# A node pass as two turns of 196 units instead of fourteen turns of 28 (one fused graph layer and mixture-of-experts kernel)

## The chip, the cores and the metric

The kernel runs on one core of a Trainium2 chip. The metric is the device time of one execution in microseconds (us). Before the change it is 3060.57 us, the median of three runs (3055.15 to 3062.44).

## What is computed

The reference takes 50,000 nodes with 768 float32 features and 25,000 edges sorted by destination, and does two things one after the other:

```
x = x + gnn(layernorm(x), src, dst, W, attn_l, attn_r, W_res)   # attention over a node's edges, + residual matmul, relu
x = x + ffn(layernorm(x)[None], moe0_*, A1_*, A2_*, G_W)[0]      # gelu(x @ W1 + b1) @ W2 + b2; 6 class tokens apart
```

The first part has a sum over edges per node (softmax weights over each node's incoming edges) and a matmul with W_res for every node, whose result goes through a relu. The second part is, for all nodes but the first six, an up-projection from 768 to 96, a gelu and a down-projection back to 768. The first six rows go through pairs of small experts with a gate.

## The kernel before, in words

Everything is written by hand for the five engines: each engine has a block of its own (`sync`, `gpsimd`, `scalar`, `tensor`, `vector`) whose instructions run in the order in which they are written, and semaphores join them. There are two passes over data. The edge pass handles 196 chunks of 128 edges in a loop of 14 chunks (`NB` turns), and writes sums per chunk to a table in HBM. A short stretch of single steps joins the sums of chunks. Then comes the node pass, which the change is about.

The node pass has `NT` = 392 units of 128 nodes. `turns(eng, NT // U, 1)` makes its turns, and the inner `for u in range(U)` is written out by Python when the kernel is built. With `U` = 28 there are 14 turns. `turns` gives the first two as Python integers (written out in the program), the rest from 2 on by `eng.Fori`, a loop with a register that all five engines run each for itself, and last a drain turn, again an integer. In the drain only stages that are still behind exist (`exists`). So 12 of the 14 turns are one body of instructions that the engines run 12 times, with 11 jumps back to its start. The body's number of instructions, as the compiled program lists them: ScalarE 183, GpSimd 152, SyncE 153, VectorE 281.

A unit t passes through stages that lie some units apart (`L_BASE` = 3 to `L_ST` = 20), so each engine works on several units at once:

- SyncE loads node rows, two units at a time, into `x_ring` (14 units deep) and transposed ones into `xt_ring` (7 deep), and stores results from `y_ring`.
- GpSimd (lines 550 to 578) prepares `g_ring`, gathers the edge sums of the unit's nodes into it (L570, an indirect DMA; nodes without edges are left out), normalises (L562), and takes reciprocal roots (L578).
- ScalarE copies transposes out of PSUM (L647), takes squares and sums for the norms (L640, L661, L678), and does the gelu (L667).
- VectorE adds the residual and the gathered sums (L1174, L1179), adds the down-projection (L1163), takes norms' statistics (L1202) and splits the hidden values (L1214).
- TensorE does in each unit six transposes (L707), the up-projection (L839), six down-projection matmuls (L851) and six residual matmuls (L860).

In the loop, the number that a semaphore is waited for depends on the turn, so it stands in a register that the engine computes. In written-out turns it is a constant. The relevant helper:

```
    yield 0
    yield 1
    with eng.Fori(2, n) as b:
        yield b
```

Of the kernel before, what the change touches and what calls it, by code (L numbers as in the profile page):

```python
# [16 lines left out]
HC = P // DH  # L17

PAIR = 2
U = 28  # L20
XR = 14
GR = 7
NT = -(-N_NODES // (P * U)) * U
# [28 lines left out]
L_BASE = 3  # L52
L_RES = 4
L_Y = 5
# [14 lines left out]
def turns(eng, n, drain):  # L69


    yield 0
    yield 1
    with eng.Fori(2, n) as b:
        yield b
    for b in range(drain):
        yield n + b

# [11 lines left out]
def at_least(eng, sem, value):  # L90

    if not isinstance(value, int) or value > 0:
        eng.wait_ge(sem, value)


def gnn_ffn_kernel(nc, x, x_cols, edges, dst_next, dst_prev, dst_ends, chunk_base, sel_heads,
# [9 lines left out]
    with ExitStack() as ctx:  # L106
# [283 lines left out]
        @block.sync  # L390
        def _(sp):

            sp.dma_start(ident[:], eye).then_inc(l_const, 16)
            sp.dma_start(w_dup[:, 0:DH], w_gnn).then_inc(l_const, 16)
            sp.dma_start(w_dup[:, DH:P], w_gnn).then_inc(l_const, 16)
            sp.dma_start(attn_sb[:], attn).then_inc(l_const, 16)
            sp.dma_start(wgv[:, :, 0:P], w_gnn_bd[:, None, :].to_broadcast([P, NC, P])).then_inc(l_const, 16)
            sp.dma_start(wr_bd[:], w_res_bd).then_inc(l_const, 16)
            sp.dma_start(w1_sb[:], w1.rearrange("(c p) h -> p c h", p=P)).then_inc(l_const, 16)
            sp.dma_start(b1_sb[:], b1.rearrange("(p a) -> p a", a=1)).then_inc(l_const, 16)  # L400
            sp.dma_start(w2_sb[0:HID, :], w2).then_inc(l_const, 16)
            sp.dma_start(w2_sb[HID:HID + 1, :], b2.rearrange("(a c) -> a c", a=1)).then_inc(l_const, 16)

            sp.dma_start(gw_sb[:], gw.rearrange("(c p) g -> p c g", p=P)).then_inc(l_cls, 16)
            sp.dma_start(a1b_sb[:], a1b).then_inc(l_cls, 16)
            sp.dma_start(cb_sb[:], chunk_base).then_inc(l_fix, 16)

            sp.wait_ge(s_rowinit, 1)
            sp.dma_start(row_d.rearrange("(p n) o -> p (n o)", p=P), row_init).then_inc(d_rowinit, 16)

            for b in turns(sp, NB, 2):
                for i in range(BODY):
                    co_ = BODY * b + i - L_AGG
                    if exists(co_, EC):
                        v = (i - L_AGG) % G
                        sp.wait_ge(s_eo, co_ + 1)
                        sp.dma_start(agg_v[ds(co_, 1)].rearrange("a p d -> p (a d)"), agg_ring[:, v, :])\
                            .then_inc(d_agg[v], 16)

            sp.wait_ge(s_ecol, EC)  # L420
            sp.wait_ge(s_tr, NBLK * EC)
            sp.wait_ge(s_ag, 2 * EC)
            sp.dma_start(row_i, dst_ends.rearrange("(o n) e -> o n e", o=1).to_broadcast([P, 2, EC])).then_inc(l_fix, 16)
            sp.dma_start(sel_sb, sel_heads).then_inc(l_fix, 16)
            sp.wait_ge(s_tab, NG)
            sp.dma_start(tab_d, tab[:]).then_inc(d_tab, 16)
            sp.wait_ge(d_tab, 16)
            for k in range(G):
                sp.dma_start(tb.rearrange("h (g k) n -> h g k n", k=G)[:, :, k, :],
                             tab_d[k * HEADS:(k + 1) * HEADS]).then_inc(l_tab, 16)  # L430
            for u in range(G):
                sp.wait_ge(d_agg[u], 16 * (EC // G))
            sp.dma_start(o_last, tail_v[:, :, P - 1, :]).then_inc(d_last, 16)
            for u in range(2):
                sp.wait_ge(d_scat[u], 16 * (EC // 2))

            for b in turns(sp, NT // U, 1):
                for u in range(U):
                    t = b * U + u
                    if u % PAIR == 0 and exists(t, NT):  # L440
                        v = u % XR
                        j = v // PAIR
                        n = 2 * b + u // XR
                        q = b * (U // PAIR) + u // PAIR
                        at_least(sp, s_y, t - XR + PAIR)
                        settle(sp)
                        sp.dma_start(x_ring[:, v:v + PAIR, :], x_v[ds(q, 1)].rearrange("q p k c -> p (q k) c"))\
                            .then_inc(d_x[j], 16)
                        at_least(sp, d_g[(u - XR) % GR], 16 * (4 * b + (u - XR) // GR + 1))
                        settle(sp)  # L450
                        at_least(sp, d_g[(u - XR + 1) % GR], 16 * (4 * b + (u - XR + 1) // GR + 1))
                        settle(sp)
                        sp.dma_start(nrow[:, v:v + PAIR], row_v[ds(q, 1)].rearrange("q p k -> p (q k)"))\
                            .then_inc(d_x[j], 16)
                    tx = t - L_XT
                    if exists(tx, NT):
                        g = (u - L_XT) % GR
                        at_least(sp, s_res, tx - GR + 1)
                        settle(sp)
                        sp.dma_start(xt_ring[:, g, :], x_cols[ds(tx, 1)].rearrange("t f c -> f (t c)"))\  # L460
                            .then_inc(d_xt[g], 16)
                    if isinstance(t, int) and t == NT + 10:
                        sp.wait_ge(s_y, NT)
                        sp.dma_start(a1_sb, a1w.rearrange("(c p) a h -> p c a h", p=P)).then_inc(l_cls, 16)
                        sp.dma_start(a2_sb[0:HID, :, :], a2w).then_inc(l_cls, 16)
                        sp.dma_start(a2_sb[HID:HID + 1, :, :], a2b.rearrange("(o a) d -> o a d", o=1)).then_inc(l_cls, 16)
                    to = t - L_ST
                    if (u - L_ST) % PAIR == 1 and exists(to, NT):
                        v = (u - L_ST) % XR - 1
                        sp.wait_ge(s_o, to + 1)  # L470
                        settle(sp)
                        lo = NCLS // PAIR if isinstance(b, int) and to == 1 else 0
                        q = b * (U // PAIR) + (u - L_ST - 1) // PAIR
                        sp.dma_start(out_v[ds(q, 1), lo:P].rearrange("q p k c -> p (q k) c"),
                                     y_ring[lo:P, v:v + PAIR, :]).then_inc(d_out[v // PAIR], 16)

            sp.wait_ge(s_clsx, PAIR)
            sp.dma_start(cls_d.rearrange("(p k) c -> p k c", k=PAIR), cls_x).then_inc(d_clsx, 16)
            sp.wait_ge(d_clsx, 16)
            sp.wait_ge(s_y, NT)  # L480
            sp.dma_start(co[:, 0, :], cls_d).then_inc(l_clsx, 16)
            for u in range(XR // PAIR):
                sp.wait_ge(d_out[u], 16 * (NT // XR))
            sp.wait_ge(s_cout, 1)
            sp.dma_start(out[0:NCLS, :], co[:, 2, :]).then_inc(d_cls, 16)
            sp.wait_ge(d_cls, 16)

        @block.gpsimd
        def _(pool):
# [49 lines left out]
            for b in turns(pool, NT // U, 1):  # L539
                for u in range(U):  # L540
# [23 lines left out]
                    if exists(tb_, NT):  # L564
                        v = (u - L_BASE) % XR
                        g = (u - L_BASE) % GR
                        pool.wait_ge(d_x[v // PAIR], 32 * (2 * b + (u - L_BASE) // XR + 1))
                        pool.wait_ge(s_base, tb_ + 1)
                        settle(pool)
                        pool.indirect_dma_start(g_ring[:, g, :], None, agg_d,  # L570
# [10 lines left out]
        def _(act):  # L581
# [50 lines left out]
            for b in turns(act, NT // U, 1):  # L632
                for u in range(U):
# [38 lines left out]
                    if u % PAIR == 1 and exists(t, NT):  # L672
                        v = u % XR
                        w = (v // PAIR + 1) % (XR // PAIR)
                        act.wait_ge(d_x[v // PAIR], 32 * (2 * b + u // XR + 1))
                        at_least(act, s_sq1, b * (U // PAIR) + u // PAIR)
                        at_least(act, s_base, t - XR + 1)
                        nc.scalar.activation(junk[:, 0, :], x_ring[:, v, :], ACT.Copy, scale=1.0 / D,  # L678
# [12 lines left out]
        def _(pe):  # L691
# [131 lines left out]
            for b in turns(pe, NT // U, 1):  # L823
                for u in range(U):
# [29 lines left out]
                    tr = t - L_RES  # L854
                    if exists(tr, NT):
                        g = (u - L_RES) % GR
                        pe.wait_ge(d_xt[g], 16 * (4 * b + (u - L_RES) // GR + 1))
                        at_least(pe, s_y, tr)
                        for i in range(NC):
                            last = nc.tensor.matmul(pair(1)[:, i * P:(i + 1) * P], xt_ring[:, g, i * P:(i + 1) * P],  # L860
# [25 lines left out]
        def _(dve):  # L886
# [265 lines left out]
            for b in turns(dve, NT // U, 1):  # L1152
                for u in range(U):
# [11 lines left out]
                    if exists(ty, NT):  # L1165
# [4 lines left out]
                        k = v % PAIR  # L1170
                        dve.wait_ge(s_res, ty + 1)
                        dve.wait_ge(s_rn, b * (U // PAIR) + (u - L_Y) // PAIR + 1)
                        dve.wait_ge(d_g[g], 16 * (4 * b + (u - L_Y) // GR + 1))
                        V.scalar_tensor_tensor(pair(1), pair(1), r_n[:, w, k:k + 1], g_ring[:, g, :],  # L1174
                                               ALU.mult, ALU.add).then_inc(s_z1, 1)
                        dve.wait_ge(s_z1, ty + 1)
                        if v % PAIR == 0:
                            at_least(dve, d_out[v // PAIR], 16 * (2 * b + (u - L_Y) // XR))
                        V.scalar_tensor_tensor(y_ring[:, v, :], pair(1), 0.0, x_ring[:, v, :], ALU.max, ALU.add,  # L1179
                                               accum_out=s_st[:, w4, k:k + 1]).then_inc(s_y, 1)  # L1180
                    q = b * (U // PAIR) + u // PAIR
# [15 lines left out]
                    if u % PAIR == 0 and exists(t, NT):  # L1197
                        v = u % XR
                        w = (v // PAIR + 1) % (XR // PAIR)
                        dve.wait_ge(d_x[v // PAIR], 32 * (2 * b + u // XR + 1))  # L1200
                        for h in range(2):
                            V.bn_stats(bn1[:, u // PAIR % 2, h, :], x_ring[:, v, h * (D // 2):(h + 1) * (D // 2)]).then_inc(s_bn1, 1)  # L1202
                    if u % PAIR == 0 and exists(t, NT):
# [102 lines left out]
```

## Time and profile before

| what | value |
|---|---|
| median of three runs | 3060.57 us |
| the profiled execution's own time | 3053.38 us |
| its span, first to last instruction | 3051.6 us |
| mean granted TensorE clock | 0.975 of full speed |
| TensorE busy | 2867.4 us, 94% |
| VectorE, GpSimd, ScalarE busy | 2484.8, 2140.6, 1829.4 us |
| node pass, about | from 1210 us to the end |

A line number such as L860 is that of the kernel before. "PE" is TensorE's matmuls, "PEld" its weight loads, DVE is VectorE, ACT ScalarE, POOL GpSimd, SPq and POOLq the engines that issue transfers. A number in brackets at a row's end is the idle time before it and what ended it; "issue" there means that the engine waited for nothing that the profile shows. An fp32 matmul counts as two records, so that the six matmuls of line 860 show as x12.

### The profile page before, as it was taken

What the parts mean: (1) busy time and instruction counts of PE and PEld (TensorE: products, weight loads), DVE (VectorE), ACT (ScalarE), POOL (GpSimd) and SP (SyncE); (2) the same over time, 40 slices, a digit from 0 to 9 for tenths busy, and PEclk for the clock granted to TensorE, in tenths of its full rate; (3) what the DMA queues carried; (4) which work ended last, traced back from release to release, by engine and by line L of the source; (5) the groups of instructions that cost most, each with busy time, mean ns of one, the idle gap of its engine ahead of it and who ended that gap; (6) DMA issues with size and microseconds to landing.
All of it is one profiled execution on the core that took longest, in us unless ns stands there. A gap on an engine that the chain in (4) does not pass through costs nothing. (4 is left out here: it accounts for less than half of the span.)

```text
span 3051.6 us, 69396 instructions
## 1 busy us (share of the span) xinstructions
PE 2867.4 (94%) x20124; PEld 2554.1 (84%) x20124; DVE 2484.8 (81%) x5828; ACT 1829.4 (60%) x3384; POOL 2140.6 (70%) x2027
## 2 busy tenths in 40 slices
PE   2999999999999984799999999999999999999998
PEld 2988888888888863688888888898988989889896
DVE  4799999999999964688878787787877888778883
ACT  1666666666666631566666666666666666666662
POOL 6766666666666500778877787787877878778782
PEclk9999999999999995799999999999999999999998
DMA  7999999988888624799988888888888888888873
GB/s 180 203 223 217 215 214 224 214 218 218 217 216 217 175 90 156 237 325 315 317 287 309 272 300 286 287 298 287 295 286 276 299 275 301 272 276 295 277 253 122
DMA packets 246672, 758.47 MB, mean 249 GB/s; under 512 B 78899, under 2 KB 81203, under 8 KB 246291
## 3 DMA queue, kind: packets, MB, share of 16 engines
q1 hardware_dynamic: 176644, 545.08, 50.4%
q0 software_dynamic: 69312, 209.33, 30.4%
q8 instruction: 136, 2.23, 0.3%
q14 instruction: 148, 1.21, 0.1%
q10 hardware_dynamic: 432, 0.62, 0.1%
HBM read 623.04 MB, written 232.17 MB: 280 GB/s over the span
## 5 line engine op out<-in xcount | busy, mean ns | idle before, releaser
L647 ACT ACTIVATE arena<-ps 128x768 f32<-128x768 f32 x392 | 317.3, 810 | 550.1 <-PE ps L707 550.0
L860 PE MATMUL ps<-wr_bd,arena 128*128 128x128 f32 x4704 | 600.3, 278 | 35.2 <-DVE arena L1179 34.1
L860 PEld LDWEIGHTS ps<-wr_bd,arena 128*128 128x128 f32 x4704 | 565.6, 194 | 43.2 <-issue 34.8
L839 PE MATMUL ps<-arena,w_sb 128*96 128x256 f32 x2352 | 580.6, 383 | 0.0
L570 POOL DMA_INDIRECT arena<-agg_scratch,nrow x392 | 438.9, 1120 | 78.1 <-issue 69.8
L1174 DVE SCALAR_TENSOR_TENSOR ps<-ps,r_n,arena 128x768 f32<-128x768 f32 x392 | 400.1, 1021 | 54.1 <-DMA arena<-agg_scratch,nrow 32.5
L839 PEld LDWEIGHTS ps<-arena,w_sb 128*96 128x96 f32 x2352 | 368.0, 165 | 85.9
L550 POOL TENSOR_SCALAR arena<-csr_neg,mv,r_n 128x768 f32<-128x768 f32 x392 | 385.9, 984 | 52.4 <-POOL r_n L578 42.1
L609 ACT ACTIVATE arena<-ps 128x512 f32<-128x512 f32 x588 | 307.5, 594 | 189.9 <-PE ps L724 188.5
L1163 DVE TENSOR_TENSOR arena<-arena,ps 128x768 f32<-128x768 f32 x392 | 363.7, 928 | 53.3 <-issue 36.5
L1179 DVE SCALAR_TENSOR_TENSOR arena<-ps,arena 128x768 f32<-128x768 f32 x392 | 375.4, 958 | 17.1
L562 POOL TENSOR_SCALAR arena<-arena,nm_n,r_n 128x768 f32<-128x768 f32 x392 | 382.1, 975 | 2.2 <-issue 1.6
L578 POOL TENSOR_TENSOR r_n<-ve_n,half 128x4 f32<-128x4 f32 x199 | 205.6, 1033 | 246.8 <-DVE ve_n L1195 246.5
L661 ACT ACTIVATE arena<-arena,s_st 128x768 f32<-128x768 f32 x392 | 364.3, 929 | 21.5 <-DVE arena L1179 21.5
L707 PE MATMUL ps<-ident,arena 128*128 128x128 f32 x2352 | 327.5, 276 | 35.4 <-issue 35.4
L851 PE MATMUL ps<-w_hi,h_hi 97*128 97x512 f32 (+1 forms) x784 | 339.3, 433 | 2.4 <-DVE arena L1163 2.4
L724 PE MATMUL ps<-ident,arena 128*128 128x128 f32 x2352 | 291.7, 274 | 48.9 <-ACT arena L595 46.9
L724 PEld LDWEIGHTS ps<-ident,arena 128*128 128x128 f32 x2352 | 271.1, 142 | 68.0 <-issue 47.2
L506 POOL DMA_INDIRECT arena<-in_x,e_slot x196 | 191.5, 977 | 168.2 <-PE ps L769 111.7
L707 PEld LDWEIGHTS ps<-ident,arena 128*128 128x128 f32 x2352 | 274.5, 143 | 37.5 <-issue 37.5
L733 PE MATMUL ps<-wgv,arena 128*128 128x130 f32 x2352 | 295.8, 275 | 0.0
L733 PEld LDWEIGHTS ps<-wgv,arena 128*128 128x128 f32 x2352 | 279.0, 191 | 0.1
(197 smaller groups left out, 5420.0 us busy)
## 6 DMA issues: line engine op xcount, KB each, us to landing
arena<-in_x SPq DMA_DIRECT2D x196, 768.0 KB, 6.2
arena<-in_x_cols SPq DMA_DIRECT2D x392, 384.0 KB, 4.7
out<-arena SPq DMA_DIRECT2D x195, 768.0 KB, 5.2
agg_scratch<-arena SPq DMA_DIRECT2D x196, 384.0 KB, 6.4
arena<-in_x,e_slot POOLq DMA_INDIRECT x392, 6.5
arena<-agg_scratch,nrow POOLq DMA_INDIRECT x392, 6.2
row_scratch<-e_slot POOLq DMA_INDIRECT x196
nrow<-row_scratch SPq DMA_DIRECT2D x196, 1.0 KB, 7.1
```

Source lines behind the costliest of these rows:

```text
L550: pool.tensor_scalar(g_ring[:, g, :].rearrange("p (c f) -> p c f", f=P), csr_neg[:, None, :].to_broadcast([P, NC, P]), mv1[:, w, 2 * (v % ...
L562: pool.tensor_scalar(n2[:, v % 2, :], y_ring[:, v, :], nm_n[:, w, k:k + 1], r_n[:, w, PAIR + k:PAIR + k + 1], ALU.add, ALU.mult).then_inc( ...
L570: pool.indirect_dma_start(g_ring[:, g, :], None, agg_d, bass.IndirectOffsetOnAxis(nrow[:, v:v + 1], 0), bounds_check=EP - 1, oob_is_err=Fa ...
L661: nc.scalar.activation(junk[:, 1, :], y_ring[:, v, :], ACT.Square, bias=s_st[:, w, k:k + 1], scale=-float(D), accum_out=q_st[:, w, 1 + k:2 ...
L707: last = nc.tensor.transpose(dst[:, c * P:(c + 1) * P], src[:, c * P:(c + 1) * P], ident[:])
L724: last = nc.tensor.transpose(ps[:, k, m % 4 * P:(m % 4 + 1) * P], src[:, v, m % NC * P:(m % NC + 1) * P], ident[:])
L733: last = nc.tensor.matmul(ft_ps[:, n // 3, n % 3, :], both_t[:, v, n * P:(n + 1) * P], wgv[:, n, :], start=True, stop=True)
L839: last = nc.tensor.matmul(ps[0:HID, 6 + v, 0:PAIR * P], w1_sb[:, i, :], t2[:, v, i, :], start=(i == 0), stop=(i == NC - 1))
L860: last = nc.tensor.matmul(pair(1)[:, i * P:(i + 1) * P], xt_ring[:, g, i * P:(i + 1) * P], wr_bd[:], start=True, stop=True)
L1163: V.tensor_tensor(y_ring[:, v, :], y_ring[:, v, :], pair(2), ALU.add).then_inc(s_o, 1)
L1174: V.scalar_tensor_tensor(pair(1), pair(1), r_n[:, w, k:k + 1], g_ring[:, g, :], ALU.mult, ALU.add).then_inc(s_z1, 1)
L1179: V.scalar_tensor_tensor(y_ring[:, v, :], pair(1), 0.0, x_ring[:, v, :], ALU.max, ALU.add, accum_out=s_st[:, w4, k:k + 1]).then_inc(s_y, 1)
```

## The change

`U` becomes 196, a number that divides the 392 units into two turns. `turns` gives both as integers, and a guard leaves out the loop where there are no more than two turns. So the node pass is written out in full, 392 units and the drain, on all five engines. The numbers waited for were written for a turn of 28 (2 rings of 14, 4 rings of 7) and are now computed from `U`. The edge pass keeps its loop. Depths of rings, stages, tiles and the computation are the same.

```diff
-U = 28
+U = 196
@@
     yield 0
     yield 1
-    with eng.Fori(2, n) as b:
-        yield b
+    if n > 2:
+        with eng.Fori(2, n) as b:
+            yield b
     for b in range(drain):
         yield n + b
@@
-                        n = 2 * b + u // XR
+                        n = U // XR * b + u // XR
@@
-                        at_least(sp, d_g[(u - XR) % GR], 16 * (4 * b + (u - XR) // GR + 1))
+                        at_least(sp, d_g[(u - XR) % GR], 16 * (U // GR * b + (u - XR) // GR + 1))
@@
-                        dve.wait_ge(d_g[g], 16 * (4 * b + (u - L_Y) // GR + 1))
+                        dve.wait_ge(d_g[g], 16 * (U // GR * b + (u - L_Y) // GR + 1))
```

The other changed lines replace `2 * b` by `U // XR * b` and `4 * b` by `U // GR * b` in the same way.

The first place is TensorE at the end of the loop's body and what follows it. In the program of before (`ps` is PSUM, `wr_bd` the residual weights, `ident` the identity of the transposes, L74 the loop):

```order
L93 REGISTER_ALU [waits d_xt2]
L860 MATMUL ps<-wr_bd,arena 128x128 [waits s_y]
L860 MATMUL ps<-wr_bd,arena 128x128 x5
L74 REGISTER_ALU
L74 COMPARE_AND_BRANCH
```

The body that it jumps back to begins with these rows:

```order
L74 ISA
L93 REGISTER_ALU [waits s_n2]
L707 MATMUL ps<-ident,arena 128x128 [waits s_te2]
L707 MATMUL ps<-ident,arena 128x128 x5
L93 ISA [waits s_te2]
L839 MATMUL ps<-arena,w_sb 96x256 [waits s_hlo]
```

In the changed program the same place (unit 83 to unit 84, where the first jump back was) reads as follows; its lines have numbers one higher:

```order
L861 MATMUL ps<-wr_bd,arena 128x128 [waits s_y,d_xt2]
L861 MATMUL ps<-wr_bd,arena 128x128 x5
L708 MATMUL ps<-ident,arena 128x128 [waits s_te2,s_n2]
L708 MATMUL ps<-ident,arena 128x128 x5
L840 MATMUL ps<-arena,w_sb 96x256 [waits s_hlo,s_te2]
L840 MATMUL ps<-arena,w_sb 96x256 x2
```

The branch, the loop's register step and the instructions that carried a wait on a register's value are gone; the waits stand on the matmuls. The matmuls and their order are unchanged.

The second place is VectorE at the same point. Before, the body's end:

```order
L1179 SCALAR_TENSOR_TENSOR arena,s_st<-ps,arena 128x768 [waits d_out4,s_z1]
L93 REGISTER_ALU [waits s_hhi]
L1214 TENSOR_TENSOR h_lo<-ps,h_hi 96x256 [waits s_down]
L74 REGISTER_ALU
L74 COMPARE_AND_BRANCH
```

and after:

```order
L1180 SCALAR_TENSOR_TENSOR arena,s_st<-ps,arena 128x768 [waits d_out4,s_z1]
L1215 TENSOR_TENSOR h_lo<-ps,h_hi 96x256 [waits s_down,s_hhi]
L1164 TENSOR_TENSOR arena<-arena,ps 128x768 [waits s_down]
L1175 SCALAR_TENSOR_TENSOR ps<-ps,r_n,arena 128x768 [waits d_g2,s_rn,s_res]
L1180 SCALAR_TENSOR_TENSOR arena,s_st<-ps,arena 128x768 [waits s_z1]
```

Here too the next unit's work follows directly, and nothing changed its place.

## Rows read from the trace of the kernel before

**Rows 1.** The page: span, busy time and instructions of each engine

```profile
span 3051.6 us, 69396 instructions
...
PE 2867.4 (94%) x20124; PEld 2554.1 (84%) x20124; DVE 2484.8 (81%) x5828; ACT 1829.4 (60%) x3384; POOL 2140.6 (70%) x2027
```

**Rows 2.** Timeline of TensorE, then windows (clock third from the end), inside a loop turn

```profile
2227.24 1.50 PE L860 MATMUL ps<-wr_bd,arena 128*128 128x128 f32 x12
2231.57 1.50 PE L860 MATMUL ps<-wr_bd,arena 128*128 128x128 f32 x12
...
2222.00:2340.00 118.00, 118.00 (x818) 106.74 (x817) 99.16 (x214) 78.94 (x160) 96.61 (x95) 1.00 0.86 296
```

**Rows 3.** Waits from 1483 to 2990 us: us in total, times, longest

```profile
DVE arena L1163 <- issue: 36.5, 11, 4.1
PE ps L707 <- issue: 35.4, 11, 4.8
ACT arena L640 <- issue: 34.4, 11, 5.1
DVE ps L1174 <- DMA arena<-agg_scratch,nrow: 18.6, 34, 1.6
```

**Rows 4.** Timeline of TensorE around one jump

```profile
2210.96 0.82 PE L707 MATMUL ps<-ident,arena 128*128 128x128 f32 x6
2211.62 1.46 PE L839 MATMUL ps<-arena,w_sb 128*96 128x256 f32 x6
...
2213.98 1.50 PE L860 MATMUL ps<-wr_bd,arena 128*128 128x128 f32 x12
2218.17 1.43 PE L707 MATMUL ps<-ident,arena 128*128 128x128 f32 x6 [2.69 <-issue]
2219.39 2.62 PE L839 MATMUL ps<-arena,w_sb 128*96 128x256 f32 x6
...
2222.90 1.28 PE L860 MATMUL ps<-wr_bd,arena 128*128 128x128 f32 x10
```

**Rows 5.** Windows around the jumps, same columns as in rows 2

```profile
1701.00:1715.00 14.00, 9.18 (x52) 7.77 (x51) 7.90 (x18) 6.01 (x12) 9.01 (x10) 0.81 0.88 304
1832.00:1845.00 13.00, 9.83 (x57) 8.42 (x56) 7.68 (x17) 5.90 (x12) 7.22 (x8) 0.87 0.84 274
...
2844.00:2856.00 12.00, 9.38 (x54) 8.04 (x53) 7.40 (x16) 5.95 (x12) 7.17 (x8) 0.86 0.76 252
```

**Rows 6.** Timeline, L707 at turns' starts; windows, second turn

```profile
1330.46 0.82 PE L707 MATMUL ps<-ident,arena 128*128 128x128 f32 x6
...
1454.42 0.82 PE L707 MATMUL ps<-ident,arena 128*128 128x128 f32 x6
...
1581.62 0.87 PE L707 MATMUL ps<-ident,arena 128*128 128x128 f32 x6 [3.08 <-issue]
...
2850.21 1.54 PE L707 MATMUL ps<-ident,arena 128*128 128x128 f32 x6 [2.62 <-issue]
...
1330.50:1454.40 123.90, 122.19 (x842) 109.96 (x840) 103.35 (x225) 83.91 (x169) 100.33 (x99) 1.00 0.90 319
```

**Rows 7.** DMA queues (packets, MB, share), the second turn, then a loop turn

```profile
q0 software_dynamic: 2249, 6.26, 14.7%
q8 instruction: 7, 0.11, 0.3%
...
q0 software_dynamic: 2380, 3.36, 9.2%
q8 instruction: 9, 0.15, 0.5%
```

**Rows 8.** Waits, the second turn, then a late loop turn

```profile
DVE ps L1174 <- DMA arena<-agg_scratch,nrow: 5.5, 7, 2.0
...
PE ps L860 <- DVE arena L1179: 1.6, 2, 1.3
...
DVE ps L1174 <- DMA arena<-agg_scratch,nrow: 1.0, 3, 0.4
```

More of the change, by code:

```diff
@@ L448, in _ @@
                             .then_inc(d_x[j], 16)
-                        at_least(sp, d_g[(u - XR) % GR], 16 * (4 * b + (u - XR) // GR + 1))
+                        at_least(sp, d_g[(u - XR) % GR], 16 * (U // GR * b + (u - XR) // GR + 1))
                         settle(sp)
-                        at_least(sp, d_g[(u - XR + 1) % GR], 16 * (4 * b + (u - XR + 1) // GR + 1))
+                        at_least(sp, d_g[(u - XR + 1) % GR], 16 * (U // GR * b + (u - XR + 1) // GR + 1))
                         settle(sp)
@@ L566, in _ @@
                         g = (u - L_BASE) % GR
-                        pool.wait_ge(d_x[v // PAIR], 32 * (2 * b + (u - L_BASE) // XR + 1))
+                        pool.wait_ge(d_x[v // PAIR], 32 * (U // XR * b + (u - L_BASE) // XR + 1))
                         pool.wait_ge(s_base, tb_ + 1)
@@ L674, in _ @@
                         w = (v // PAIR + 1) % (XR // PAIR)
-                        act.wait_ge(d_x[v // PAIR], 32 * (2 * b + u // XR + 1))
+                        act.wait_ge(d_x[v // PAIR], 32 * (U // XR * b + u // XR + 1))
                         at_least(act, s_sq1, b * (U // PAIR) + u // PAIR)
@@ L856, in _ @@
                         g = (u - L_RES) % GR
-                        pe.wait_ge(d_xt[g], 16 * (4 * b + (u - L_RES) // GR + 1))
+                        pe.wait_ge(d_xt[g], 16 * (U // GR * b + (u - L_RES) // GR + 1))
                         at_least(pe, s_y, tr)
@@ L1177, in _ @@
                         if v % PAIR == 0:
-                            at_least(dve, d_out[v // PAIR], 16 * (2 * b + (u - L_Y) // XR))
+                            at_least(dve, d_out[v // PAIR], 16 * (U // XR * b + (u - L_Y) // XR))
                         V.scalar_tensor_tensor(y_ring[:, v, :], pair(1), 0.0, x_ring[:, v, :], ALU.max, ALU.add,
@@ L1199, in _ @@
                         w = (v // PAIR + 1) % (XR // PAIR)
-                        dve.wait_ge(d_x[v // PAIR], 32 * (2 * b + u // XR + 1))
+                        dve.wait_ge(d_x[v // PAIR], 32 * (U // XR * b + u // XR + 1))
                         for h in range(2):
```

## The prediction

> **What bounds the kernel now.** I read the page first: span, busy shares, clock. TensorE is busy for 94% of the span [rows 1], ahead of every other engine. Then I looked at the node pass unit by unit in the timeline. In an undisturbed stretch, the residual matmuls of line 860 start at 2227.24 and again at 2231.57 us [rows 2]: one unit of 128 nodes takes 4.33 us. TensorE is busy for all 118.00 us of the stretch from 2222 to 2340 us at a granted clock of 1.00, while VectorE has 99.16 us of work, GpSimd 96.61 and ScalarE 78.94 [rows 2]. So the pace of a unit is TensorE's own work. VectorE is the next, at 84%. If every unit ran at this pace, 28 of them would take 28 x 4.33 = 121.3 us.
>
> Next I asked the view of waits for the part with the loop turns, 1483 to 2990 us [rows 3]. TensorE waits in it for 35.4 us ahead of line 707, in 11 pieces, and the view names "issue": no semaphore and no data. VectorE (L1163, 36.5 us) and ScalarE (L640, 34.4 us) have exactly 11 such gaps too. The node pass has 14 turns of 28 units, the first two are written out, and 12 run as a loop, which jumps back 11 times. L707, L1163 and L640 are the first instructions of the loop's body on these engines. One such place in the timeline [rows 4]: the last matmuls of the body (L860) start at 2213.98, and the first of the next turn (L707) at 2218.17, after 2.69 us without work. VectorE and ScalarE stand still at such a place for 3.3 and 3.1 us on average (36.5/11, 34.4/11). The next L860 group starts at 2222.90: this unit took 8.92 us in place of 4.33.
>
> Of the 4.6 us too many, 2.7 are the gap. The rest is the clock. Behind the gap the six transposes take 1.43 us and the six up-projection matmuls 2.62 us, which took 0.82 and 1.46 us a unit earlier [rows 4]. The view by windows has a granted clock of 0.86 in the 12 us around this place, the same as in the last row; so do seven of the eleven windows, one has 0.87 in 13 us, one 0.81 in 14 us, and two 1.00 (rows 5 show the second, the third and the last). Between the jumps it is 1.00 [rows 2]. A fall after a gap is thus one to the lower level, 1.2 GHz, for a few us.
>
> **The change, part by part.** U goes from 28 to 196 and the number of units stays 392, so there are two turns, both written out, and no loop in this pass. The order of the instructions on each engine stays the same; what goes are the jumps, the register arithmetic and register waits.
>
> (1) The gaps at the 11 jumps. TensorE: 35.4 us [rows 3]. The longest is 4.8 us, the mean 3.2. TensorE is the bound on both sides of the gap, so they lie on the path in full. That the other engines' gaps go too brings nothing more: theirs lie beside TensorE's.
>
> (2) The lower clock behind them. In each window, what is lost is its length times (1 minus the clock): 14 x 0.19 + 13 x 0.13 + 7 x 12 x 0.14 = 2.7 + 1.7 + 11.8 = 16.2 us [rows 5]. With no gap, nothing lets the clock fall: in the written-out turn and inside all turns it is 1.00. The Trainium skill (TensorE: Matmul & The Clock Gate, "What's actually happening") says that the clock's default is the low level and activity lifts it; the trace agrees, low only behind gaps.
>
> (3) Register arithmetic and nops that carry waits. The second turn, written out, has none of them; TensorE is busy for 122.19 of its 123.90 us [rows 6], and inside the loop's turns for 118.00 of 118 [rows 2]. So TensorE's queue hides them already, and they are worth 0. Where that cover ran dry they would stand as idle pieces ahead of matmuls between the jumps, and there are none.
>
> (4) Instruction fetch. The second turn, which is written out, fetched 7 packets of 16 KB on q8, a loop turn 9 [rows 7]; I take this queue for TensorE's, whose program is by far the longest. So the loop's body is already fetched anew in every turn, and straight code asks for no more: 0.11 MB beside the 6.26 MB of the gather queue alone. Worth 0, with the bound in (5).
>
> (5) What a written-out turn really costs. The first L707 of the second turn starts at 1330.46 and that of the third at 1454.42 [rows 6]: 123.96 us, 2.7 above 121.3. In it VectorE waited for gathers of line 570 seven times, 5.5 us in all, of which 1.6 us got through to TensorE (L860) [rows 8]. In a late loop turn this wait is 1.0 us [rows 8]: early nodes have more edges, and the gather queue moved 6.26 MB in the second turn and 3.36 in the late one [rows 7]. So later written-out turns should come close to 121.3. The loop turns: from the first L707 behind the first jump, 1581.62, to the one behind the last, 2850.21, are ten turns [rows 6], 126.86 us each. Against 123.96 the change brings 2.90 x 11 = 32 us; against 121.3 it brings 5.56 x 11 = 61 us. The sum of parts, 35.4 + 16.2 = 51.6 us, counts only what happens at the jumps. It lies between, nearer to the upper bound, as it should with gather waits that shrink, and I take it.
>
> The profiled execution took 3053.4 us (span 3051.6), so it would take 3053.4 - 51.6 = 3001.8. The median of the runs shown is 3060.6, 7.2 us above it, and would go to 3009. The upper bound leaves room for slightly more, so I write 3008.
>
> A rule of the skill, weighed. The gap at a jump is 3.2 us in the mean [rows 3]. The Trainium skill (Advanced Engine Details and Errata, "Control Flow Timing") gives some 51 ns for a jump and 108 ns for a compare-and-branch. By those the change would be worth 11 x 0.16 = 1.7 us, an estimate, and nothing measurable. The trace decides against it here. Another page (Runtime: NRT & Kernel Launch, "Instruction fetch mechanics") says that a taken jump out of the small window of instructions waits for a fetch, which would make the gap part of the jump. No row shows the fetch itself standing behind the gap. By the same page, ScalarE's body (183 instructions, at the page's 64 bytes each) would lie inside that window and its jump would not wait; the trace has 11 gaps there.
>
> **The rivals.** A measurement of this kernel tells about 0.3% (9 us) from no change.
>
> *The pauses gave slack that comes back as gather waits.* The jump halts VectorE and GpSimd too, while transfers go on landing. Without it, VectorE may wait oftener for line 570's gathers (34 times, 18.6 us, in the loop part [rows 3]), with TensorE behind it. Against it: inside the turns the pace of 4.33 us holds far from the last jump. If each of 11 turns lost as much as the second one, with gathers as heavy as there, the gain would be the lower bound of 32 us: 3029 against the median. Chance 0.12.
>
> *The pauses are not the jump's.* If something else with a period of 28 units caused them (a wrap of rings, a burst of transfers), they would stay: 3060.6, no change. The rings wrap every 7 or 14 units, and there is no gap ahead of L707 at 1330.46, where the second written-out turn begins, nor at 1454.42, where the loop is entered [rows 6]. By the Trainium skill's jump times above it would be 3059. Chance 0.03.
>
> *Straight code is fetched too slowly: slower.* The place is the end of each 16 KB packet of TensorE's stream: 0.11 MB in 7 packets a turn [rows 7], 84 in twelve turns. If each stopped the engine as a jump does, 35.4/11 = 3.2 us, this would cost 269 us, and the result would be 3009 + 269 = 3278. It decides the sign from 51.6/84 = 0.61 us a packet. The second turn has 7 packets and 2.7 us too many, 1.6 of which are gathers; the other 1.1 us give 0.16 us a packet. So this needs fetches that behave worse further on than in the first two turns. Chance 0.03.
>
> *The gain is larger:* each turn saves up to 5.56 us, as loops also cause the follow-up waits behind a jump: 3053.4 - 61 = 2992, or 3000 against the median. Chance 0.1.
>
> **How the numbers follow.** The forecast proper, 3002 to 3016, has 0.72. The larger gain has 0.1, the returned gather waits 0.12, no change 0.03, slower 0.03. The range from 2998 to 3022 holds the forecast, the larger gain and part of the gather case. Faster by over 0.3% 0.94, same 0.03, slower 0.03.
>
> **What the profile after would show.** Right: no "issue" gap of some 3 us ahead of the transposes or of VectorE's and ScalarE's first instructions from the third turn on; units at 4.33 us through the whole pass; the clock at 1.00 from a few units behind the pass's start to its end, so a mean clock of about 0.98 (16 of 3050 us more at full speed); the span near 3000; TensorE's busy time lower by the lower clock's share (about 16 us); the same number of matmuls, and about as many instruction packets. Wrong on (4) would be idle "issue" pieces spread at every fourth unit or so; wrong on (5) a sum of L1174's waits for gathers far above 33 us with L860 waiting behind. The forecast fails if the written-out second turn is not typical of the 336 units behind it, or if the timed runs' pauses differ from those of the profiled one.

## The result, and the profile after

The changed kernel takes 3009.86 us (median of four runs, 3007.71 to 3011.33), the kernel before 3061.51 us (four runs). The ratio is 0.9834 with a 95% interval of 0.9817 to 0.9851: faster by 51.6 us, 1.7%. The forecast was 3008.

The page of the changed kernel, as in [rows 1], with TensorE's clock over the 40 slices:

```profile
span 3009.5 us, 65141 instructions
...
PE 2853.7 (95%) x20124; PEld 2542.5 (84%) x20124; DVE 2488.2 (83%) x5828; ACT 1842.5 (61%) x3384; POOL 2120.1 (70%) x2027
...
PEclk9999999999999997699999999999999999999998
```

The matmuls are as many as before (20124), and what is missing are 4255 records, of the engines' own bookkeeping. TensorE's busy time fell by 13.7 us with the same work: matmuls at the lower clock take longer ([rows 4]), and fewer of them do. The mean granted clock is 0.983, before it was 0.975.

The timeline of TensorE around one of the old jumps' places, unit 83 to unit 84 (compare L707 at 1581.62 in [rows 6], and [rows 4]):

```profile
1587.41 1.50 PE L861 MATMUL ps<-wr_bd,arena 128*128 128x128 f32 x12
1588.75 0.82 PE L708 MATMUL ps<-ident,arena 128*128 128x128 f32 x6
1589.40 1.46 PE L840 MATMUL ps<-arena,w_sb 128*96 128x256 f32 x6
...
1591.82 1.57 PE L861 MATMUL ps<-wr_bd,arena 128*128 128x128 f32 x12
```

From one group of residual matmuls to the next it is 4.41 us here, and there is no idle piece in brackets. The windows view of the node pass from its first units to its last says the same in one row (busy times of PE, PEld, DVE, ACT and POOL, then clock, DMA share, GB/s). Of the kernel before:

```profile
1440.00:2989.00 1549.00, 1508.98 (x10287) 1357.23 (x10288) 1261.98 (x2739) 1012.95 (x2052) 1229.28 (x1200) 0.99 0.83 286
```

and of the changed one:

```profile
1440.00:2950.00 1510.00, 1506.27 (x10362) 1356.38 (x10361) 1275.51 (x2760) 1034.16 (x2069) 1241.78 (x1209) 1.00 0.84 295
```

TensorE stood still for 40.0 of 1549 us before and for 3.7 of 1510 us now, with the clock at its higher level throughout that stretch now. The view of waits of the changed kernel from 1465 to 2950 us, to be read beside [rows 3] and [rows 8]:

```profile
DVE ps L1175 <- DMA arena<-agg_scratch,nrow: 33.0, 61, 1.5
...
PE ps L861 <- DVE arena L1180: 3.1, 10, 0.8
```

The three lines with 11 "issue" gaps of about 3 us are gone. VectorE waits more often for gathers (33.0 us where it was 18.6). The view shows 3.1 us in which TensorE stood still for VectorE. That is not all that reaches it: a unit can also take longer without an idle piece, as the 4.41 us above show. The experiment without gathers puts the whole at 10.5 us.

The node pass from its first to its last group of residual matmuls took 1778.6 us before and 1728.0 now, 50.6 us less. The profiled spans differ by only 42.1 us, because in the profiled execution of before the node pass began at 1210.74 us and in that of the changed kernel at 1222.27 (what follows the pass took 62.2 and 59.2 us). What this is, the last experiment asks.

### The profile page after: what moved, and what is told of

It is laid out like the page before. It is cut to its first block and busy times, and to the rows that moved or that the text cites. A ratio compares the mean times of both kernels' runs of the same rounds, so it can differ in the third digit from the quotient of the medians.

```text
span 3009.5 us, 65141 instructions
## 1 busy us (share of the span) xinstructions
PE 2853.7 (95%) x20124; PEld 2542.5 (84%) x20124; DVE 2488.2 (83%) x5828; ACT 1842.5 (61%) x3384; POOL 2120.1 (70%) x2027
## 5 line engine op out<-in xcount | busy, mean ns | idle before, releaser
L861 PE MATMUL ps<-wr_bd,arena 128*128 128x128 f32 x4704 | 598.4, 277 | 36.0 <-DVE arena L1180 34.6
L861 PEld LDWEIGHTS ps<-wr_bd,arena 128*128 128x128 f32 x4704 | 562.8, 193 | 45.7 <-issue 43.2
L840 PE MATMUL ps<-arena,w_sb 128*96 128x256 f32 x2352 | 571.6, 379 | 0.0
L551 POOL TENSOR_SCALAR arena<-csr_neg,mv,r_n 128x768 f32<-128x768 f32 x392 | 387.5, 989 | 50.6 <-POOL r_n L579 39.9
L725 PEld LDWEIGHTS ps<-ident,arena 128*128 128x128 f32 x2352 | 271.9, 142 | 70.0 <-issue 51.2
L616 ACT ACTIVATE arena<-ps 128x780 f32<-128x780 f32 x196 | 161.2, 822 | 212.6 <-PE ps L734 122.5
```

The source lines that it names most:

```text
L551: pool.tensor_scalar(g_ring[:, g, :].rearrange("p (c f) -> p c f", f=P), csr_neg[:, None, :].to_broadcast([P, NC, P]), mv1[:, w, 2 * (v % ...
L725: last = nc.tensor.transpose(ps[:, k, m % 4 * P:(m % 4 + 1) * P], src[:, v, m % NC * P:(m % NC + 1) * P], ident[:])
L840: last = nc.tensor.matmul(ps[0:HID, 6 + v, 0:PAIR * P], w1_sb[:, i, :], t2[:, v, i, :], start=(i == 0), stop=(i == NC - 1))
```

## The experiments

Times are medians in us. 3009.9 is the changed kernel, 3061.5 the one before (3063.4 and 3066.0 in the two later groups of runs). "The pass" is the node pass in the profiled execution, from its first to its last group of residual matmuls: 1728.0 us in the changed kernel. It was worked out from the traces for every run, and so were the clock records and the counts of records below.

**How many jumps.** Seven turns of 56 units, five of them in the loop:

```diff
-U = 196
+U = 56
```

> The changed kernel with U = 56: seven turns of 56 units, five of them as a loop, so 4 jumps back in place of 11 or none. If the cost belongs to the jump (51.6 us / 11 = 4.7 us each, whatever the body's length): 3010 + 4 x 4.7 = 3029 us. If it belonged to work in the loop's units (register arithmetic and register waits, 280 of 336 units still in a loop): 3010 + 51.6 x 280/336 = 3053 us. If the pauses came from a period of 28 units: 3061.

Measured: 3036.64, ratio to before 0.9914 (0.9884 to 0.9944). That is 26.8 us above the changed kernel for 4 jumps, where 19 were expected. In its profile the node pass is 20.8 us longer (1748.8 against 1728.0), 5.2 a jump, close to the 4.7 expected; of the other 6 us, 4.5 lie outside the pass in the two profiles, and five runs spread from 3028 to 3044. The waits view has four gaps ahead of TensorE's transposes (from 1440 to 3000 us):

```profile
DVE arena L1164 <- issue: 14.6, 4, 3.7
ACT arena L641 <- issue: 12.7, 4, 3.7
...
POOL arena L551 <- issue: 12.0, 4, 4.0
PE ps L708 <- issue: 11.3, 4, 3.3
```

GpSimd, which had no such gap at the jumps of the kernel before, now has one of 3.0 us per jump: its loop body has doubled too. SyncE, which issues transfers, goes on 5.6 to 5.8 us after its branch here and 0.3 us after it before. So the cost goes with the jumps, not with units in a loop (3053) and not with a period of 28 units (3061).

**Which engine's jump.** Four kernels mix the two forms. In each, the node pass of some engines is as before and that of the others written out; the order of work is the same. The edit is a local constant at the head of an engine's block, here for TensorE alone in the loop:

```diff
 def _(pe):
+    U = 28
```

> Only TensorE's node pass is written out; the other four engines keep the loop of 28 units. If TensorE's own gap is the whole cost and the others' gaps lie beside it, as the prediction says: near 3010 us. If VectorE's and ScalarE's gaps of 3 us and more reach TensorE through the semaphores (it is at most a unit ahead of VectorE): TensorE waits for VectorE at each jump of the others instead, some 2 to 3 us and the lower clock behind it, so 3035 to 3055 us.

> The reverse: only TensorE keeps the loop of 28 units, the other four are written out. If TensorE's own gap is the whole cost: 3061 us, as before. If the cost needed the other engines' gaps too (VectorE behind its own fetch just when TensorE comes back): below 3061 by 5 us or more. 3010 would say that TensorE's jump is harmless.

> Only VectorE keeps the loop of 28 units (281 instructions in its body), the other four are written out. With only TensorE written out the time was 3065 us, with only TensorE in the loop 3046 us, so the others' jumps alone are enough. VectorE stands still for 3 to 4 us at a jump and has some 0.7 us of slack a unit. If it is the one: 3040 to 3060 us. If it was ScalarE: near 3010.

> Only ScalarE keeps the loop of 28 units (183 instructions, or about 239 with the ones that read its accumulator). It stands still for some 3 us at a jump and is busy for 67% of a unit, but TensorE's transposes wait for its copy of the unit before. If such a gap reaches TensorE: 3030 to 3045 us. If ScalarE's slack takes it: 3010 to 3015.

| in the loop of 28 | time | above the changed kernel | ratio to before, interval |
|---|---|---|---|
| all five (before) | 3061.5 | 51.7 | |
| all but TensorE | 3065.0 | 55.2 | 1.0015 (0.9997 to 1.0033) |
| TensorE alone | 3046.4 | 36.5 | 0.9945 (0.9930 to 0.9960) |
| VectorE alone | 3050.1 | 40.2 | 0.9955 (0.9938 to 0.9971) |
| ScalarE alone | 3019.6 | 9.8 | 0.9859 (0.9843 to 0.9876) |
| none (changed) | 3009.9 | 0 | |

The parts add up to far more than the whole: 36.5 + 40.2 + 9.8 = 86.5 against 51.7. By ratios the three are 34, 37 and 8 us, still 79. By the pass they are 28.8, 32.9 and 6.5 us, 68.2 in sum, against 50.6 for all five. The gaps lie beside each other. Writing out TensorE alone, the engine that bounds the pass, brings nothing that its ten runs show; 3065.0 also lies above both ranges that were expected. (Its profiled execution was the fastest of the ten, and its pass, 1768.3 us, was 6 to 10 us shorter than in the two profiles of before.) In that kernel's waits (same stretch) the gaps of the others stand on TensorE's rows as waits for VectorE, 11 times each:

```profile
DVE arena L1168 <- issue: 33.5, 11, 4.3
...
PE ps L855 <- DVE arena L1168: 18.0, 11, 2.8
```

With only VectorE in the loop TensorE waits for it in the same way (and at L861, 9.8 us in 21 pieces):

```profile
PE ps L852 <- DVE arena L1165: 13.8, 11, 1.4
```

ScalarE's gaps are there as well when it alone loops (L642, 25.9 us in 11), but its slack takes most of them: 0.9 us a jump comes through by the medians, 0.6 by the pass.

With only TensorE in the loop, the 11 units that hold a jump are too long by 42.5 us, more than the pass grew. All its other units from the third turn on are too long by less than 2 us in sum, where those of the changed kernel are by 12.4. VectorE waits for gathers there for 4.9 us where it was 33.0. This fits pauses of TensorE that give the gathers time, with some 10 us won back; no run separates it further. These other units also keep TensorE's register waits, which thus cost nothing that can be seen.

**A near jump.** The changed kernel with a small loop at the 11 places, on all five engines:

```diff
+                    if t % 28 == 0 and 84 <= t < NT:
+                        with pe.Fori(0, 2):
+                            pe.nop(nofuse=True)
```

> The changed kernel with a tiny loop of two turns (its body one empty instruction) on all five engines at the 11 unit boundaries where the kernel before jumped back: a jump to an instruction just behind, everything else written out. If the cost of a jump is the fetch of instructions that are no longer in the engine: 3010 to 3013 us, no issue gaps. If the jump in itself stops the engine for 3 to 5 us (draining, register arithmetic): 3061 us.

Measured: 3017.31, ratio 0.9852 (0.9836 to 0.9868). Its node pass takes 1726.7 us from first to last group of L861's matmuls, against 1728.0 without the small loops: nothing. The median is 7 us higher, above the 3010 to 3013 expected; the two profiles differ by 4.1 us ahead of the pass and 2.9 behind it. The cause was not found, and the two ratios' intervals overlap. So the jump in itself is harmless.

**A body too long to stay, in the other pass.** The edge pass's jumps had cost nothing. Now its body holds two turns:

```diff
+    with eng.Fori(0, (n - 2) // 2) as c:
+        yield 2 * c + 2
+        yield 2 * c + 3
```

> The changed kernel, with the edge pass's loop carrying two turns of 14 chunks in its body, so that it jumps back 5 times in place of 11; the order of work is the same. The edge pass's jumps cost TensorE nothing that shows (300.00 us busy of 300), and no instruction packet is fetched from 300 to 1060 us, so its body seems to stay in the engine. If what costs is a body too long to stay there: the doubled body (915 instructions of TensorE in the compiled list, the node pass's had 646) is fetched anew at each jump, 5 x 3.2 to 4.8 us more: 3026 to 3034 us, with issue gaps in the edge pass and q8 packets in it. If what costs is something of the node pass, or the jump in itself: 3010 us or a little less.

Measured: 3042.64, ratio 0.9927 (0.9903 to 0.9951): 32.8 us slower than the changed kernel for 5 jumps in place of 11, and 9 us above the upper end expected. The node pass begins at 1257.9 us in place of 1222.3, and takes no longer than before. The waits from 300 to 1115 us have the gap (L736 is the edge pass's first transposes):

```profile
PEld ps L736 <- issue: 23.7, 5, 6.2
PE ps L736 <- issue: 21.7, 5, 5.8
```

The clock records have the lower level for 23.9 us behind these five gaps, a loss of 12.0 us. With the 21.7 that makes 33.7, near the measured 32.8; the expectation had priced the gaps alone.

The DMA view of the edge pass, 300 to 1060 us, is the fetch itself. In the kernel before it lists two queues and no instruction queue:

```profile
q0 software_dynamic: 26355, 107.97, 67.3%
q1 hardware_dynamic: 20117, 54.93, 18.5%
```

With the doubled body it lists both instruction queues (packets, MB, share):

```profile
q8 instruction: 57, 0.93, 0.6%
q14 instruction: 34, 0.28, 0.2%
```

So the loop body of 14 chunks stays in the engines; the doubled one is fetched again in each turn, and TensorE and VectorE wait for it at each jump. (VectorE goes on 4.7 to 6.4 us after its branch, and 0.3 us with the single body; ScalarE, GpSimd and SyncE go on after at most 0.3 us with either.) The trace's records of TensorE's sequencer tell the same at each jump. How long the compare-and-branch took there, worked out from the trace:

```
kernel          pass   jumps back   compare-and-branch on TensorE, ns
before          edge   11           207 to 247
before          node   11           3970 to 6337
doubled body    edge   5            5183 to 7372
56 units        node   4            3866 to 4727
near jumps      node   11           217 to 368
```

At the first jump of the kernel before the record begins at 1576.6 and ends at 1581.4 us, and TensorE's queued matmuls last to 1578.5. The DMA view has a 16 KB instruction packet in just this stretch, 1578 to 1582 us (first lines), and only a small one on the other queue in the five us from 1572 to 1577 (last line):

```profile
q8 instruction: 1, 0.02, 2.5%
q14 instruction: 2, 0.02, 1.9%
...
q14 instruction: 1, 0.01, 0.8%
```

It is so at every jump: in the kernel before, during each of the 11 records of TensorE's branch exactly one 16 KB packet starts on q8, and one to four of 8 KB on q14. With only TensorE in the loop, the 11 records (3.7 to 5.2 us) have one packet each on q8. With only VectorE or only ScalarE in the loop, the time from its branch to its next instruction (2.8 to 3.1 us, and 2.6 to 3.8) has at least one packet on q14 each time. So q8 serves TensorE, as the prediction took it, and the wait behind the jump is for instructions.

**A gap without a jump.** The changed kernel, with one wait more on TensorE at the 11 places:

```diff
+                    if t % 28 == 0 and 84 <= t < NT:
+                        pe.wait_ge(s_y, t - L_RES)
```

> The changed kernel, without jumps, but with one more wait on TensorE at the same 11 places: its transposes wait until VectorE has finished line 1180 of the unit just before, which opens a gap of some 2.3 us or more. It measures what a gap costs with no jump and no fetch. If a gap also lowers the clock behind it, as the prediction's step (2) has it: gap plus up to 1.7 us each, 11 x (2.3 to 4) = 25 to 44 us, so 3035 to 3054 us and a mean clock below 0.983. If the lower clock came with the fetch: the gaps alone, clock 0.983.

Measured: 3053.84, ratio 0.9964 (0.9950 to 0.9978), 44 us above the changed kernel; the node pass takes 1769.8 us, 41.8 more. The waits view has the new gaps:

```profile
PE ps L708 <- DVE arena L1182: 26.5, 11, 3.0
```

They are 26.5 us in sum. The trace's clock records have the lower level for 27.3 us between 1450 and 2990 us, behind 8 of the 11 gaps, and none in the changed kernel. Half speed for 27.3 us loses 13.7 us, and 26.5 + 13.7 = 40.2, near the 41.8. A gap of 2.4 us thus costs 3.8 here, with no jump and no fetch. The same sum holds for the jumps: in the first profile of before 35.4 us of gaps and half of 34.1 us at the lower level make 52.5, where the pass took 50.6 us longer than in the changed kernel.

**Do gather waits eat part of the gain?** Two kernels leave the gathered sums out:

```diff
-    bounds_check=EP - 1, oob_is_err=False).then_inc(d_g[g], 16)
+    bounds_check=0, oob_is_err=False).then_inc(d_g[g], 16)
```

> The changed kernel, whose node pass leaves out the gathered edge sums: the bound of line 571's gather is 0, so that no row is fetched (the instruction stays). In the changed kernel's trace VectorE waits 34.2 us for gathers from 1440 to 2960 us, and in the one before 18.6 us in its loop part. If these waits are what makes written-out units longer than 4.33 us (15 us over the pass): 2995 us. If other things do: 3008 or more.

> The same left out in the kernel before: no row is gathered in the node pass. The units outside of the jumps took some 13 us too many there: 3048 us if gathers are their cause. The difference of the two kernels would then be 53 us or slightly more, against 51.6 us with gathers: the part of the gain that is given back as gather waits is 1 to 5 us.

Measured: 2998.09 written out, 3050.93 with the loop, so 52.8 us between them, against 51.7 us with gathers (as ratios 0.9947 - 0.9782 = 1.65% against 1.66%). The intervals leave some 6 us of doubt on such a difference, so the traces say more. In the written-out one, units after the third turn's start are too long by 1.9 us in sum, where they were by 12.4, so 10.5 us are the gathers'; with the loop 3.3 and 9.8 (outside the jumps), 6.5 us. So gathers do make most of what a unit takes above 4.33 us, in both kernels. Their part is 4.0 us larger in the changed kernel, and its units away from the jumps are too long by 2.6 us more (3.5 by the second profile of before). So some 3 to 4 us of the gain were given back to gathers.

**The edge pass written out too**

```diff
+def written(eng, n, drain):
+    for b in range(n + drain):
+        yield b
```

> The changed kernel with the edge pass written out as well (14 turns of 14 chunks and the drain, no loop left). Its loop bodies stay in the engines and its jumps take 0.2 us of TensorE's sequencer each, covered by the queue: 3010 us if the fetch of a body that doesn't stay is the cost, at most 2 us less. If each jump had its price as in the node pass: 3010 - 11 x 4.7 = 2958 us. Slower, 3013 to 3020, if straight code's fetches cost the edge pass something.

Measured: 3009.03, ratio 0.9814 (0.9797 to 0.9832). No difference from the changed kernel that the runs show: from 300 to 1060 us TensorE is busy for 760.00 of the 760 us here, and for 759.61 in the changed kernel. The one written out fetched 49 packets on q8 there, the looped one none, and neither waited. So writing out the edge pass adds nothing to the gain.

**The kernel before, once more**

> The kernel before, unchanged, profiled once more. In its first profile the edge pass's first jump of VectorE was some 11 us earlier than in every written-out version, and the whole execution took 3053.4 us against a median of 3061.6. If that is a matter of the execution: a span near 3060 us and the node pass's first residual matmul near 1222 us, with the node pass as long as before (1778.6 us from its first to its last unit). If it belongs to the program: 1211 us again.

Measured: 3065.35. Its first residual matmul starts at 1228.60 us, in the first profile it was 1210.74:

```profile
1228.60 2.93 PE L860 MATMUL ps<-wr_bd,arena 128*128 128x128 f32 x12 [0.47 <-ACT arena L628]
```

and its node pass takes 1774.2 us. So the stretch ahead of the node pass varies by 18 us between executions of one program. Of the 18 us, 12 are there at the edge pass's first jump (TensorE's branch at 226.1 and at 238.1 us), later turns take 76.3 us on average in both, and 5 come in the stretch that joins the chunks. The first profile is the odd one: in the other kernels whose edge pass is the same this branch lies between 236.9 and 241.4 us. The cause was not found. The gaps at the jumps are shorter in this execution:

```profile
PE ps L707 <- issue: 30.7, 11, 4.2
```

With 34.1 us at the lower level again, gaps and clock make 47.8 us. With this profile as the base the pass has become shorter by 46.2 us, with the first by 50.6.

## Why the prediction was right, point by point

- **The bound.** Right. TensorE is busy for 1506.27 of 1510 us in the pass, and a unit takes 4.33 us.
- **(1) The gaps, 35.4 us.** Right in size: TensorE's idle time in the pass fell by 40.0 - 3.7 = 36.3 us. The sentence that the other engines' gaps, once gone, bring "nothing more" is wrong. With TensorE written out and the others in the loop the time is 3065.0; writing out the others too brings all of the 55 us. With TensorE left in the loop, writing out the others brings 15 us. The gaps do lie beside each other, but VectorE's alone cost 40.2 us and TensorE's alone 36.5, so neither engine's gaps are the whole cost. The forecast was not hurt by this, because the change took the loop from all five engines at once.
- **(2) The lower clock, 16.2 us.** Right in mechanism: the gap without a jump had the clock fall too. In size it lies between 13.7 us (TensorE's busy time over the whole span) and 17 us (the trace's clock records of before have the lower level for 34.1 us of the loop part, those of the changed kernel for none; half of that is lost). (The "six" up-projection matmuls of L839 are three; six is the number of their records.)
- **(3) Register waits, 0.** Right: with 280 of 336 units still in a loop the cost went with the four jumps (20.8 us of the pass), and with TensorE alone in the loop its units away from the jumps are too long by less than 2 us in sum.
- **(4) Fetch of straight code, 0.** Right. The page has 113 packets on q8 where it was 136, and 116 on q14 where it was 148, so the straight code asks for fewer; the prediction had "about as many". The Trainium skill (Runtime: NRT & Kernel Launch, "Instruction fetch mechanics") has engines stream sequential code unnoticed and wait for a fetch at a jump out of what they hold; the runs agree with both halves (3.7 us of idle time with 87 packets, one packet on q8 in each of 11 branch records). They don't agree with the size of what is held: ScalarE's body would lie inside it, as the prediction noted, and ScalarE waits 3.1 to 6.0 us at each jump.
- **(5) A written-out turn.** Later turns came between 121.6 and 123.3 us, 122.4 on average, a good 1 us above the bound of 121.3. The sum of parts, 51.6 us, was the measured 51.6 us, helped by luck: the pass became shorter by 50.6 or 46.2 us, by which profile of before one takes, and the rest lies in the varying stretches ahead of it and behind it.
- **The rivals.** "Gather waits return": VectorE's waits did rise from 18.6 to 33.0 us, and some 3 to 4 us of the gain went that way, not the 20 us of this rival. "The pauses are not the jump's": fell with the 56 units. "Fetched too slowly": fell with 87 packets of straight code from 1440 to 2960 us and 3.7 us of idle time in all. The Trainium skill's times for a jump (Advanced Engine Details and Errata, "Control Flow Timing") fit a near jump in size only: at the small loops the branch records have 56 to 67 ns on VectorE, 45 on ScalarE and 217 to 368 on TensorE. They leave out the fetch. VectorE's and ScalarE's records do too: at the far jumps they have 67 to 72 and 45 ns, but the next instruction follows 3.0 to 4.3 and 3.1 to 6.0 us later, where it is 0.2 us at a near jump.
- **How long a body may be** was bracketed by counting every record of a turn, register and semaphore instructions included. (The compiled list quoted above counts otherwise.) TensorE holds the edge pass's body (1287 records) and not the node pass's (1803). VectorE holds 299 (edge pass) and not 375 (node pass). ScalarE holds 292 (the doubled edge pass) and not 307 (node pass). GpSimd holds 278 and not 546.
- **Left open:** why SyncE's body of 307 records stays in the kernel before (it goes on 0.3 us after its branch) while ScalarE's of 307 doesn't. What a gap of GpSimd or SyncE costs was not measured by itself.

## What to carry to other kernels

In these runs a loop's jump cost nothing that shows as long as the body stayed in the engine (0.2 us on TensorE's sequencer, covered by its queue). When it didn't stay, the jump waited for a fetch: 4 to 7 us on TensorE's sequencer, 3 to 6 on the others. To see which, ask the DMA view for instruction packets inside the loop, and the waits view for "issue" gaps that come as often as the jumps. Shorten or write out the body on all engines that have the gap, since one that is left can keep most of the cost (36 of 52 us for TensorE, 40 for VectorE, 10 for ScalarE). And price a gap on TensorE with the clock that it loses behind it.

## What the runs showed of the hardware that I had not expected

The edge pass's loop made no instruction packet at all in 760 us, so bodies do stay. On ScalarE they stop doing so between 292 and 307 records a turn, on VectorE between 299 and 375. A gap of 2.4 us on TensorE cost 3.8 us, since the clock was at 1.2 GHz for a while behind 8 of the 11. And an unchanged program began its node pass at 1210.7 us in one execution and at 1228.6 in another.
